# Self-attention step: the output projection and the scores, interleaved by halves

## The reference

```python
q = (x @ Wq.T + bq).reshape(b, l, h, hd).transpose(0, 2, 1, 3)
k = (x @ Wk.T + bk).reshape(b, l, h, hd).transpose(0, 2, 1, 3)
v = (x @ Wv.T + bv).reshape(b, l, h, hd).transpose(0, 2, 1, 3)
scores = jnp.einsum('bhqd,bhkd->bhqk', q, k) / math.sqrt(hd)
scores = jnp.where(causal, scores, -jnp.inf)
att = jax.nn.softmax(scores, axis=-1)
out = jnp.einsum('bhqk,bhkd->bhqd', att, v)
return out.transpose(0, 2, 1, 3).reshape(b, l, d) @ Wo.T + bo
```

## Time and profile before

| | us |
|---|---|
| median of three runs | 1754.99 (1753.63 to 1756.02) |
| the profiled execution, its own time | 1755.72 |
| its span | 1753.8 |
| PE busy | 1688.0 |
| DVE busy | 1266.0 |
| POOL busy | 958.2 |
| ACT busy | 919.6 |

### The profile page before, as it was taken

How to read it: one execution, slowest core, us unless ns; L and a number is a source line. 1 busy time by engine, 2 the same in 40 slices (tenths; PEclk the granted TensorE clock), 3 DMA queues, 4 the chain that set the end, 5 groups by cost and what they waited for, 6 DMA issues and landing times. The chain is left out here.

```text
span 1753.8 us, 39041 instructions
## 1 busy us (share of the span) xinstructions
PE 1688.0 (96%) x15461; PEld 963.1 (55%) x15461; DVE 1266.0 (72%) x2051; ACT 919.6 (52%) x1518; POOL 958.2 (55%) x875
## 2 busy tenths in 40 slices
PE   7899998899999999999999999999889999999997
PEld 5666674455555555555555555555455555455553
DVE  6778776788888888888888888888785444344445
ACT  7777673656464645455555545465742333333334
POOL 5565664556464636455555556464734555455545
PEclk9999999899999999999999999999999999999999
DMA  5531223112112314123222122131166778887658
GB/s 164 136 83 43 71 63 80 61 57 89 67 67 73 109 43 137 51 95 99 73 73 94 41 92 78 37 109 37 69 231 208 147 152 226 231 199 151 119 97 300
DMA packets 88897, 190.68 MB, mean 109 GB/s; under 512 B 14800, under 2 KB 33744, under 8 KB 86672
## 3 DMA queue, kind: packets, MB, share of 16 engines
q1 hardware_dynamic: 65232, 130.72, 22.4%
q0 software_dynamic: 22912, 57.32, 16.1%
q10 hardware_dynamic: 576, 0.14, 0.0%
HBM read 124.95 MB, written 63.21 MB: 107 GB/s over the span
## 5 line engine op out<-in xcount | busy, mean ns | idle before, releaser
L1134 POOL TENSOR_TENSOR xa_sc<-xa_sc,xa_rs 128x1024 f32<-128x1024 f32 x32 | 60.8, 1901 | 375.7 <-DVE xa_rs L1394 375.7
L1123 POOL TENSOR_TENSOR xa_xs<-xa_xs,sn 128x512 f32<-128x512 f32 x160 | 232.2, 1451 | 46.2 <-ACT xa_xs L1175 46.1
L288 PE MATMUL bank<-xhl,front_h 128*128 128x512 f16 x640 | 244.1, 381 | 11.1 <-DVE front_l L670 9.9
L290 PE MATMUL bank<-xhl,front_l 128*128 128x512 f16 x640 | 244.1, 381 | 0.0
L289 PE MATMUL bank<-xhl,front_h 128*128 128x512 f16 x640 | 244.0, 381 | 0.0
L1128 POOL TENSOR_TENSOR xa_rr<-xa_x,xa_xs 128x512 f32<-128x512 f32 x160 | 233.6, 1460 | 12.7 <-DVE xa_x L1285 0.2
L2040 POOL DMA_INDIRECT scratch_y<-raw_front,moe_to x79 | 125.3, 1586 | 148.9 <-DVE mo_zl L2094 120.8
L288 PE MATMUL bank<-out_h,xa_oh 128*128 128x512 f16 x512 | 194.4, 380 | 11.8 <-DVE xa_ol L1267 8.1
L290 PE MATMUL bank<-out_h,xa_ol 128*128 128x512 f16 x512 | 194.3, 379 | 0.0
L289 PE MATMUL bank<-out_l,xa_oh 128*128 128x512 f16 x512 | 194.3, 379 | 0.0
L1174 ACT ACTIVATE xa_xs<-bank 64x512 f32<-64x512 f32 x160 | 95.0, 593 | 140.5 <-PE bank L290 124.8
(11 more groups left out here) (320 smaller groups left out, 4666.8 us busy)
## 6 DMA issues: line engine op xcount, KB each, us to landing
xa_rawc<-in_ew SPq DMA_DIRECT2D x32, 768.0 KB, 5.4
moe_ring<-scratch_w SPq DMA_DIRECT2D x16, 1536.0 KB, 9.1
scratch_w<-xa_chunk_h SPq DMA_DIRECT2D x32, 384.0 KB, 2.3
scratch_w<-xa_chunk_l SPq DMA_DIRECT2D x32, 384.0 KB, 3.3
raw_front<-in_xwq SPq DMA_DIRECT2D x8, 1024.0 KB, 7.9
raw_out<-in_xwo SPq DMA_DIRECT2D x8, 1024.0 KB, 5.5
scratch_y<-acc SPq DMA_DIRECT2D x6, 1024.0 KB, 6.1
acc<-in_x POOLq DMA_DIRECT2D x4, 1024.0 KB, 7.5
```

Of the source, the lines that this page charges most:

```text
L288: pe.matmul(out_ap, ah, bh, start=start and m == 0, stop=False)
L290: mm = pe.matmul(out_ap, al, bh, start=False, stop=stop and m == n - 1)
L1123: PO.mark(pool.tensor_tensor(xr, xr, sn[:, :].rearrange("p (a s) -> p a s", a=1) .to_broadcast([P, QT // S, S]), ALU.mult), f"sm{r}", st)
L1134: PO.mark(pool.tensor_tensor(s4, s4, rs[:, :, :].rearrange("p h (t a) -> p (h t) a", a=1) .to_broadcast([P, 16, S]), ALU.mult), "nm", st)
```

## The change

`output` is cut in two: `output_part` takes the feature groups that it is to sum, and the first half (groups 0 and 1, six matmuls) opens the sum in bank 6 that the second half (groups 2 and 3, six matmuls) closes. `scores` takes the token tiles: the call with tiles 0 and 1 also writes the mask, the call with tiles 2 and 3 also carries the marks s0 to s3. In steps 5 to 15 the order is now: half of w, mask and scores of two tiles, half of w with its mark, scores of the other two tiles. The waits for `ko`, `ql` and `sb3` stand, as before, ahead of the mask, and so behind six matmuls of w instead of twelve. In the other steps the order is unchanged, and so is the count of instructions on every engine.

```diff
+                    def output_part(tile, bank_, gs):
+                        c, tok = tile // TQ, tokens(tile % TQ)
+                        return three_pass(pe, bank_[:, :], [(oh[:, slot(c * NG + g), tok], ol[:, slot(c * NG + g), tok],
+                                                             wo_h[:, g, :], wo_l[:, g, :]) for g in gs], start=gs[0] == 0, stop=gs[-1] == NG - 1)
+
                     def output(tile, bank_, name, st):
-                        c, tok = tile // TQ, tokens(tile % TQ)
-                        PE.mark(three_pass(pe, bank_[:, :], [(oh[:, slot(c * NG + g), tok], ol[:, slot(c * NG + g), tok],
-                                                              wo_h[:, g, :], wo_l[:, g, :]) for g in range(NG)]), name, st)
-
-                    def scores(st, also=()):
-
-                        for h in range(2):
+                        PE.mark(output_part(tile, bank_, range(NG)), name, st)
+
+                    def scores(st, ts, also=()):
+
+                        for h in range(2 if ts[0] == 0 else 0):
...
-                        for t in range(TQ):
+                        for t in ts:
...
-                        for j, mm in zip(J4, ends):
+                        for j, mm in zip(J4, ends if ts[-1] == TQ - 1 else ()):
                             PE.mark(mm, f"s{j}", st, also if j == 3 else ())
...
-                            output(tile, home["w"], "w", st)
+                            output_part(tile, home["w"], range(NG // 2))
...
-                        scores(st)
+                        scores(st, range(TQ // 2))
+                        if tile is not None:
+                            PE.mark(output_part(tile, home["w"], range(NG // 2, NG)), "w", st)
+                        scores(st, range(TQ // 2, TQ))
```

## The result

The changed kernel took 1761.59 us (median of 5 runs, 1760.37 to 1766.19) against 1754.99 (1752.27 to 1756.68). The ratio is 1.0040, 95% interval 1.0028 to 1.0052, so 4.9 to 9.1 us slower. The forecast was 1763, in 1759 to 1766. The profiled execution took 1760.37, the fastest of the five; its span is 1758.5, 4.7 us above the 1753.8 of before.

The account below looks back on a forecast made before the run. TensorE's own instruction list was taken to bound steps 5 to 15. Eight ordinary steps (4.2 us), step 7 (1.25), step 11 (1.24) and step 15 (1.2) add 7.9 us, giving 1763 us, range 1759 to 1766.

Parts of the forecast that it names:

- The bound: Steps 5 to 15: TensorE's own instruction list is the time, and no wait exists that the new order could fill.
- Switches: Between w and scores, twice a step: 0.095 us into the mask, 0.12 back to w, together 0.21 a step (0.1 to 0.25).
- The add: Before each step's transposes: the residual add, now less covered, makes PE wait 0.30 us; 0.42 + 0.69 + 0.06 from w's last matmul.
- What passes on: Steps 5 to 15: transposes and next key product queue behind the add, so the ordinary step's whole 0.52 us passes on.
- Steps 7 and 11: Instruction-fetch stalls in the scores, now after 34 matmuls; steps longer by 1.25 and 1.24 us, each between 0.52 and 1.8.
- Step 15: Mask after six matmuls of w waits 1.0 us for VectorE's late `ql`; step 1.2 us longer.
- The sum: Steps 5 to 15: 4.2 + 1.25 + 1.24 + 1.2 = 7.9 us, giving 1763 us; chance 0.64.
- (a): Steps 5 to 15: second score part covers the add (sum 4.6, 1759.6 us) or switches are free (5.6, 1760.6); chance 0.13.
- (b): More fetch stalls: steps 5, 9, 13 up to 0.5 us each, 7 and 11 0.5 more each; 1765.5 us; chance 0.13.
- (c): Not slower: over 4.4 of the 7.9 us taken up behind the stage; all gives 1755, with luck 1752.6; chance 0.10.

Follow-up runs that it names:

- only the mask between: Changed kernel with only the mask between the halves of w and all four score tiles behind the second half; 1758.61 us against 1755.18, ratio 1.0019.
- half the add: Changed kernel with the residual add of steps 5 to 15 on 256 of 512 columns; 1765.21 us, ratio 1.0065, a total the study calls unusable.
- short maximum: Kernel before, with each step's first row maximum on VectorE over half of its columns; 1754.90 us against 1755.18, ratio 1.0003.
- second profile: Changed kernel measured and profiled once more, without edits; 1764.44 us (6 runs) against 1753.99, ratio 1.0052.
- second pair: Profiles of both kernels, unedited, taken once more: changed 1764.44 us (6 runs) against 1753.99, ratio 1.0052; before, one run, 1758.12.

## Why the prediction was right, and where it was not

*The bound.* TensorE's list does set the time in steps 5 to 15, and no wait existed that the new order could fill. But the reading that PE runs there without a gap was wrong: 0.23 to 0.26 us a step were waits for VectorE's softmax chain. The earlier trace rows does not name them, ended before them.

*Switches.* Forecast 0.095 and 0.12; they are 0.11 (w of six matmuls 1.40 to the mask, against 6 x 0.215) and 0.15 (two token tiles 0.55 to w, against 0.40). Right, a little too small; the row on the transposes, 0.15, was the better neighbour than the row on 64 columns. (Behind the mask alone or one token tile the way back costs 0.11 to 0.12.) The Trainium skill, "TensorEngine Tiling (Array Packing)", Key Properties, says that a change of the tiling mode drains TensorE; the trace agrees in that every change costs, in either direction, but no run here shows that it is a drain, and the estimate of 0.11 for both together is under half of the 0.26 measured.

*The add.* Last matmul of w to L859: 1.16 us, forecast 1.17. Right.

*What passes on.* Here a step of the prediction failed: "Behind that wait the transposes and the key product of the next step are queued, so all of it passes on", with "VectorE's softmax ... moves by less than PE and becomes no bound". VectorE was already a bound, hidden in the softmax transposes. What it gained on TensorE came back: 0.33 a steady step instead of 0.52. The runs with only the mask between, with half the add and with the short maximum show it from three sides.

*Steps 7 and 11.* The mechanism was right: the stall now lies after 34 matmuls of mask and scores (16, 16 and 2 of the 8 whose other six follow), where it was after 28, and it comes with the bias load; in step 11 it moved from 22 to 28. The changed kernel's PE timeline in step 7, first profile:

```profile
129.53 0.53 PE L876 MATMUL bank<-sa_maskb,sa_identb 32*64 32x512 bf16 x16
...
131.81 0.26 PE L885 MATMUL bank<-sa_kx,sa_ql 32*64 32x128 f16 x6 [1.59 <-issue]
```

The size varies by more than the forecast's bounds: over a steady step, 1.72 and 1.28 in the first profile, 2.08 and 3.37 in the second, 2.07 and 1.35 in the kernel that has only step 15 undone. Where the place has stayed (two profiles of before, mask only between) it is 1.07 to 1.61. The means are 1.98 and 1.18, so 0.8 each; the forecast had 0.7 above the ordinary step. In the first profile it was only 0.1 and 0.2. The stalls themselves are 1.59 and 1.10 us there and 1.95 and 1.92 in the second profile, where 2.0 to 2.5 were to be seen. What scatters is the packet: the bias load was issued 0.6 to 0.7 us earlier against the step, close to the 0.52 of the forecast, but the packet came 1.1 and 1.25 us earlier in the first pair of profiles and 0.2 and 0.5 in the second. Why it does is open.

*Step 15.* Forecast 1.2, measured 17.64 - 16.53 = 1.11 in both pairs of profiles. Right.

*The sum.* From the start of w in step 5 to L859 of step 15 the first pair of profiles gives 5.0 us: (272.32 - 98.99) - (267.01 - 98.15) = 4.47, and 0.56 of step 5. The second pair gives 7.52 + 0.56 = 8.1. The forecast of 7.9 lies between, and the medians say 6.6 and 10.5. It was too high by 0.19 in each of eight steps, 1.5 us, and a clock that falls after a stall was not in it. For steps 7 and 11 together it had 2.5 us more than before; the first pair has 0.9, the second 3.9. So the mechanism was right but for what passes on, and that the total came out near the middle owes something to luck: one term 1.5 us too high, and one that came out 1.6 us lower than forecast in one pair and 1.4 higher in the other. What is behind the stage moved by no more than it moves between two runs (1486.8 and 1486.7 us before, 1486.2 and 1487.7 changed).

*The rivals.* (a) is out: the wait for the add is in all eleven steps, and the switches cost. The 5.0 us of the first pair lie near its 4.6 for other reasons, 0.23 a step paid back and two short stalls. (b) did not come in its main part: steps 5, 9 and 13 have no fetch stall in either profile of the changed kernel. (c) did not come either, as the part behind step 15 kept its length to 1.5 us.

## What to carry to other kernels

The work between the last matmul into a bank and the next write to it is cover for the engine that empties the bank; moving part of that work ahead exposes that engine. In this kernel, putting short matmuls of another shape into a run of full ones cost about 0.11 us on the way in and 0.11 to 0.15 on the way out, each time. In a timeline of matmuls, check that an engine is gapless by the distances between starts, against the same instructions elsewhere, not by brackets or busy time: the gaps of 0.07 and 0.16 us found here were 0.23 us a step. A delay on the bounding engine can be paid back by a second engine that was nearly the bound, so ask for both what their distance becomes.

## What the hardware showed that was not expected

- TensorE ran out of instructions in steps 1 to 4, 7 and 11. In every stall of 0.5 us and more that the trace puts down to issue, up to step 15 in all 13 profiles, a packet of 16 KB of the instruction queue had moved 2.2 to 2.8 us ahead of the resumption. With the bias loads left out, the packets of steps 7 and 11 move 1.9 to 2.8 us earlier and the stalls are gone; steps 1, 2 and 4 still have theirs.
- After a stall of 1.92 us the granted clock fell to 0.50 until the second half of w was through; after one of 1.95 us in the same profile, and after 1.59 and 1.10 us in the first, the matmuls of w kept their 0.215. With the half add it fell after one of 1.05 us.
- TensorE can wait without a bracket in the trace: 16.41 against 16.67 us a step with only VectorE's work cut.
